# Layer 0's cross attention: the rotary turn of queries and keys moved from two TensorE products to a VectorE shuffle and a GpSimd addition

## What is computed

```python
q = (layernorm(x) @ Wq + bq).reshape(B, 100, 16, 16)
k = (ctx @ Wk + bk).reshape(B, 361, 16, 16)
v = (ctx @ Wv + bv).reshape(B, 361, 16, 16)
def _rotate_half(x):
    d = x.shape[-1] // 2
    return jnp.concatenate([-x[..., d:], x[..., :d]], axis=-1)
q = q * cos + _rotate_half(q) * sin
k = k * cos + _rotate_half(k) * sin
scores = einsum('bqhd,bkhd->bhqk', q, k) / sqrt(16)
scores = where(mask == 0, -1e30, scores)
x = x + einsum('bhqk,bkhd->bqhd', softmax(scores), v) @ Wo + bo
```

## Time and profile before

| | |
|---|---|
| median of 3 runs | 1614.06 us |
| lowest and highest run | 1605.64 and 1620.24 us |
| profiled execution, first to last instruction (span) | 1598.2 us |
| PE, DVE, ACT, POOL busy, share of the span | 90%, 48%, 41%, 9% |
| mean granted TensorE clock over the span | 0.927 |
| l0x begins, about | 166.7 us from the span's start |

### The profile page before, as it was taken

One profiled execution on the slowest core, in us unless ns is written; L12 is line 12 of the kernel. 1 busy time (PEld: TensorE's weight loads), 2 busy tenths in 40 slices (PEclk: granted clock), 3 DMA queues, 4 the chain that ended last, 5 costly groups with the idle time before them and its releaser, 6 DMA issues. The chain is left out here.

```text
span 1598.2 us, 31910 instructions
## 1 busy us (share of the span) xinstructions
PE 1442.3 (90%) x12578; PEld 1101.1 (69%) x12578; DVE 771.4 (48%) x1744; ACT 655.8 (41%) x1696; POOL 147.9 (9%) x167
## 2 busy tenths in 40 slices
PE   7999999989878899999999987998995897799897
PEld 6776667866546668777999965667884565588632
DVE  4666437755555437650000057630004587377565
ACT  3443225643256335623444424632222676156300
POOL 3000010000010110003111300021005000300000
PEclk9999999999976989999999987899997998789999
DMA  6000222001100230045899300083503000330100
GB/s 203 2 1 1 66 40 40 3 22 34 43 1 1 65 68 3 3 161 204 310 342 346 101 11 21 2 320 110 184 16 81 1 1 2 65 49 3 64 1 21
DMA packets 43581, 120.28 MB, mean 75 GB/s; under 512 B 11695, under 2 KB 28204, under 8 KB 37920
## 3 DMA queue, kind: packets, MB, share of 16 engines
q1 hardware_dynamic: 32304, 60.67, 12.7%
q0 software_dynamic: 8256, 55.02, 10.2%
q10 hardware_dynamic: 2880, 2.62, 0.5%
HBM read 95.89 MB, written 11.00 MB: 67 GB/s over the span
## 5 line engine op out<-in xcount | busy, mean ns | idle before, releaser
L756 PE MATMUL wide<-early_kt,early_q 32*100 32x361 f32 x512 | 111.1, 523 | 1.5 <-issue 0.9
L2215 ACT ACTIVATE l1f_hidden<-wide,l1f_pack 128x128 f32<-128x128 f32 x160 | 58.8, 368 | 78.0 <-PE wide L2154 68.1
L113 PE MATMUL summed<-ident 128*128 128x128 f32 x360 | 53.7, 320 | 39.0 <-PEq L66 39.0
L2317 DVE TENSOR_TENSOR l1f_out<-summed,l1f_pack 128x256 f32<-128x256 f32 x20 | 8.5, 424 | 156.7 <-PE summed L2162 156.7
L113 PEld LDWEIGHTS summed<-ident 128*128 128x128 f32 x360 | 51.8, 233 | 43.2 <-issue 43.2
L2154 PEld LDWEIGHTS wide<-l1f_rt,l1f_pack 128*128 128x128 f32 x640 | 74.5, 192 | 1.7 <-issue 0.8
L2154 PE MATMUL wide<-l1f_rt,l1f_pack 128*128 128x128 f32 x640 | 74.8, 275 | 0.6 <-ACT l1f_rt L2205 0.6
L2162 PE MATMUL summed<-l1f_pack,l1f_hidden 128*128 128x256 f32 x320 | 72.4, 379 | 0.0
L1148 DVE TENSOR_REDUCE l3x_mx<-wide 100x2 f32<-100x722 f32 x64 | 57.9, 907 | 17.1 <-PE wide L756 17.0
L2750 DVE COPY l2f_out<-summed 100x512 f32<-100x512 f32 x8 | 5.5, 691 | 125.5 <-PE summed L2650 125.5
L1148 DVE TENSOR_REDUCE l0x_mx<-wide 100x2 f32<-100x722 f32 x64 | 57.8, 907 | 16.7 <-PE wide L756 16.6
(11 more groups left out here) (588 smaller groups left out, 3396.5 us busy)
## 6 DMA issues: line engine op xcount, KB each, us to landing
l2f_w<-l2f_w_dram SPq DMA_DIRECT2D x16, 1024.0 KB, 13.6
ctxt<-ctxt_dram SPq DMA_DIRECT2D x4, 1083.0 KB, 18.1
l1f_sorted_x<-l1f_zeros SPq DMA_DIRECT2D x4, 640.0 KB
l1f_rows<-l1f_sorted_x SPq DMA_DIRECT2D x20, 128.0 KB
l1f_sorted_y<-l1f_out ACTq DMA_DIRECT2D x20, 128.0 KB, 9.1
l0f_w<-l0f_w_dram SPq DMA_DIRECT2D x18, 128.0 KB
l1f_shared<-l1f_shared_dram SPq DMA_DIRECT2D x1, 2180.0 KB
l3f_we<-l3f_we_dram SPq DMA_DIRECT2D x1, 2048.0 KB
```

Of the source, the lines that this page charges most:

```text
L113: pe.matmul(net.summed[:, 1, 0:P], net.ident[:], net.ident[:], start=True, stop=True)
L756: pe.matmul(wide[0:S, i, 0:SKV], q4[R * i:R * (i + 1), g % 2, b, g // 2, :], kt[R * i:R * (i + 1), g % 2, b, g // 2, 0:SKV], start=True, s ...
L2215: act.activation(hidden[:, f, 0:P], wide[:, f % 4, 0:P], ACT.Gelu, bias=b1_of(pack[:, n % SLOTS, :], f)).then_inc(sem["h_ready"], 1)
L2317: dve.tensor_tensor(out[:, n % 2], summed[:, n % 2, 0:E], b2_of(pack[:, n % SLOTS, :]), ALU.add).then_inc(sem["y_ready"], 1)
```

## The change

Rotation no longer uses TensorE. `rotate(kind, b)` on VectorE takes a whole turn (a batch of keys, or half of the queries, both m): it multiplies by a table of sines that already holds the signs, then by the cosines, waits for its own writes, and exchanges rows d and d + 8 of every head with one `stream_shuffle` over both m (722 or 800 columns) into a third buffer `moved`. GpSimd adds `with_cos` and `moved` (line 999 after the change) and writes keys straight to `kd`. For queries it adds in place (line 1002), then multiplies by `some`, which now holds the scale too, in two instructions (line 1007). The three buffers hold two turns each, so VectorE waits before turn n until GpSimd has finished turn n-2. The swap matrix and its transfer are gone, the ScalarE copies of rotated keys are gone, and ScalarE waits for GpSimd's last addition before it writes exponentials into l0x_pt. The units kr and qr are gone, so there are 25 units in place of 45. l1x and l3x are not touched.

```diff
-        for t in range(B + 1):
-            if t < B and not fresh:
+        for t in range(B):
+            if not fresh:
                 order += [("k", t, m) for m in range(KC)]
-            if rope and t >= 1:
-                order += [("kr", t - 1, m) for m in range(KC)]
...
-                    else:
-                        raw = unit["k" if kind == "kr" else "q", b, m]
-                        cols = SKV if kind == "kr" else COLS
-                        pe.wait_ge(unit_free[raw % 4], raw // 4 + 1)
-                        pe.matmul(bank[:, 0:cols], net.ident[:], with_cos[:, cell(*what), 0:cols], start=True, stop=False)
-                        last = pe.matmul(bank[:, 0:cols], swap[:], with_sin[:, cell(*what), 0:cols], start=False, stop=True)
...
 # ScalarE, ahead of the exponentials
                 if rope:
                     values(B - 1)
+                    act.wait_ge(sem["rotated"], len(turns_of))
...
 # GpSimd
+                def rotated(kind, b):
+                    n = place_of[kind, b]
+                    pool.wait_ge(sem["moved"], n + 1)
+                    if kind == "k":
+                        pool.tensor_tensor(kd[:, b, :, 0:SKV], with_cos[:, n % 2, :, 0:SKV], moved[:, n % 2, :, 0:SKV], ALU.add).then_inc(sem["rotated"], 1)
+                        pool.drain().then_inc(sem["k_ready"], KC)
+                        return
+                    pool.tensor_tensor(with_cos[:, n % 2], with_cos[:, n % 2], moved[:, n % 2], ALU.add)
+                    if b == 0:
+                        pool.wait_ge(sem["some_ready"], 1)
+                    pool.drain()
+                    for m in range(KC):
+                        last = pool.tensor_tensor(qt[:, b * HALF:(b + 1) * HALF, m, :], with_cos[:, n % 2, m].rearrange("p (b s) -> p b s", b=HALF),
+                                                  some[:, b * HALF:(b + 1) * HALF].unsqueeze(2).broadcast_to([P, HALF, S]), ALU.mult)
+                    last.then_inc(sem["rotated"], 1)
+                    pool.drain().then_inc(sem["q_ready"], KC)
...
+                if rope:
+                    for what in turns_of:
+                        rotated(*what)
+                        if what == ("k", 1):
+                            spread_keys(0)
+                        if what == ("k", 3):
+                            spread_keys(1)
+                        if what[0] == "q":
+                            spread_queries(what[1])
+                    spread_keys(2)
...
 # VectorE
+                def rotate(kind, b):
+                    n = place_of[kind, b]
+                    if n >= 2:
+                        dve.wait_ge(sem["rotated"], n - 1)
+                    for m in range(KC):
+                        u = unit[kind, b, m]
+                        dve.wait_ge(sem["unit_psum"], u + 1)
...
+                        dve.scalar_tensor_tensor(out=to_sin, in0=got, scalar=shift, in1=by_sin, op0=ALU.add, op1=ALU.mult)
+                        dve.scalar_tensor_tensor(out=to_cos, in0=got, scalar=shift, in1=by_cos, op0=ALU.add, op1=ALU.mult).then_inc(unit_free[u % 4], 1)
+                    dve.drain()
+                    dve.stream_shuffle(moved[:, n % 2, :, at], with_sin[:, n % 2, :, at], HALF_TURN).then_inc(sem["moved"], 1)
...
-                        dve.tensor_scalar(some[:], some[:], 0.0, None, ALU.is_gt)
+                        dve.tensor_scalar(some[:], some[:], 0.0, SCALE, ALU.is_gt, ALU.mult).then_inc(sem["some_ready"], 1)
```

More of the change, by code:

```diff
@@ L638, in rows_of @@
             return CH if c < NCH - 1 else LAST
-        def cell(kind, b, m):
-            return (KC * b + m) % 4 if kind in ("k", "kr") else 4 + m
+        turns_of = []
+        for t in range(B):
+            turns_of.append(("k", t))
+            if t in (2, 3):
+                turns_of.append(("q", t - 2))
+        place_of = {what: n for n, what in enumerate(turns_of)}
+        HALF_TURN = [i + D // 2 if i % D < D // 2 else i - D // 2 for i in range(32)]
         def values_of(b, c):
@@ L654, in _ @@
                 if rope:
[L655 removed]
+                    load_weights(sp, net, [(cos[:], dram["rope_cos"]), (sin[:], dram["rope_sin"])], sem["rope_loaded"])
                 if gate:
@@ L815, in project_context @@
                     pe.wait_ge(sem["wk_loaded"], 32 if biases else 16)
[L816 to L819, removed]
-                                project(("k", t, m))
+                    for t in range(B):
+                        net.context.wait(pe, t)
+                        for m in range(KC):
+                            project(("k", t, m))
                         if t == 1:
@@ L836, in project_context @@
                             values(t)
-                        if rope and t in (3, 4):
-                            for m in range(KC):
-                                project(("qr", t - 3, m))
                         if t in (2, 3):
@@ L897, in keys @@
                 def keys(b, m):
-                    u = unit["kr" if rope else "k", b, m]
+                    u = unit["k", b, m]
                     act.wait_ge(sem["unit_psum"], u + 1)
-                    if biases and not rope:
+                    if biases:
                         act.activation(kd[:, b, m, 0:SKV], wide[:, u % 4, 0:SKV], ACT.Identity, bias=bk[:, m:m + 1]).then_inc(unit_free[u % 4], 1)
@@ L923, in gated @@
                     last.then_inc(sem["v_ready"], 1)
-                for t in range(B + 1 if rope else B):
+                for t in range(B):
                     if rope and t == 1:
                         values(0)
-                    if rope and t >= 1:
-                        for m in range(KC):
-                            keys(t - 1, m)
                     if not rope and not fresh:
@@ L1138, in _ @@
                         dve.reciprocal(gates[:], gates[:]).then_inc(sem["gate_ready"], 1)
-                    if rope and t in (3, 4):
-                        for m in range(KC):
-                            rotated_queries(t - 3, m)
                     if t in (2, 3):
-                        for m in range(KC):
-                            queries(t - 2, m)
+                        if rope:
+                            rotate("q", t - 2)
+                        else:
+                            for m in range(KC):
+                                queries(t - 2, m)
                 def highest(n, pair):
@@ L3504, in _layouts @@
     angle = (np.arange(SKV, dtype=np.float32)[None, :] * inv[r % (D // 2)][:, None]).astype(np.float32)
-    d["rope_cos"], d["rope_sin"] = np.cos(angle), np.sin(angle)
-    swap = np.zeros((P, P), np.float32)
-    for p in range(P):
-        lower = r[p] < D // 2
-        swap[p + D // 2 if lower else p - D // 2, p] = -1.0 if lower else 1.0
-    d["rope_swap"] = swap
+    to_lower = np.where(r < D // 2, np.float32(1), np.float32(-1))
+    d["rope_cos"], d["rope_sin"] = np.cos(angle), np.sin(angle) * to_lower[:, None]
     rows = np.minimum(np.arange(PADKV), SKV - 1)
```

64 lines of the change are left out of this document (17 added, 47 removed).

## The result

The changed kernel takes 1600.69 us (median of 14 runs, 1591.53 to 1604.32) against 1614.99 us of the kernel before in 14 runs (1605.64 to 1623.16). The ratio is 0.991, with a 95% interval of 0.989 to 0.993: 14.3 us faster. The forecast was 23.7 us faster. The direction was right, the gain about three fifths of what was forecast, and the time lies inside the stated range.

A forecast was written before the change was run, and what follows sets the result against it. TensorE was taken to bound l0x's projection and the attention behind it. Removed products -24.8, hand-over +0.7 and the reduction to `some` +0.4 gave -23.7 us, so 1590.4 us, ratio 0.985; range 1580 to 1604.

The forecast's parts named there:

- The removed products: TensorE's rotation passes in l0x's projection: eight key batches and two query halves removed, 24.8 us saved.
- the hand-over's two readings: Last projection unit before l0x's first score: VectorE reads it twice, 0.59 us each, adding 0.7 us (0.5 to 1.2).
- VectorE's own time: l0x's projection: VectorE needs 3.3 us per key turn against TensorE's 5.0, 6.8 against 7.7 with queries; cost 0.
- GpSimd's additions or the shuffle cost twice the rows: Rival in l0x's projection: GpSimd needs 50 us in 45 and starts 4 us late; +9, 1599 us; chance 0.05.
- its own sign: Wrong if l0x's first product to first score exceeds 50 us, or is 46 with the end moving much less than 23.
- The sign that it named for GpSimd: In l0x's projection, VectorE waiting ahead of its products would point to GpSimd.
- GpSimd's "Cost: 0": l0x's projection: GpSimd's additions, multiplications and transfers sum to 29 us in 45; 2 us lateness is covered, costing nothing.
- The reduction to `some`: At the transposes of x, two shuffles ahead make it 1.1 us late; 0.4 us of waiting (0 to 1.1).
- The clock rival: TensorE's clock falls to 1.2 GHz at l0x's hand-over to attention, 7 us lost; 1597.4 us; chance 0.13.
- VectorE and GpSimd stand in each other's way: Rival in l0x's projection: SBUF-reading operations hold each other off; +9.2, so -14.5 us, 1599.6 us; chance 0.10.
- the middle rivals: Three cases around l0x's projection and hand-over, at 1597.4, 1599.6 and 1599 us; chances 0.13, 0.10 and 0.05.
- the port rival: VectorE and GpSimd exclude each other in l0x's projection, 4.6 us late twice; -14.5 us, 1599.6 us; chance 0.10.

The follow-up runs named there:

- e4: Changed kernel with SP issuing all l0x key and query transfers and VectorE normalising before the first rotation; ratio to before 0.9846, first product to first score 46.37 us.
- e1: Changed kernel with SP issuing all of l0x's key and query transfers, GpSimd none; ratio to before 0.9873, first product to first score 50.03 us.
- e7: As e4, but GpSimd does each key addition twice; one run, l0x's first product to first score 46.37 us.
- e2: Changed kernel with GpSimd's transfers of key batches 2 and 3 issued after the queries' second half; one run, first product to first score 49.80 us.
- e8: Changed kernel with a semaphore wait replacing the drain between GpSimd's query addition and multiplications; one run, first product to first score 51.95 us.
- e3: Changed kernel with GpSimd's first addition waiting until VectorE has normalised all eight inputs; one run, first product to first score 50.80 us.
- e0: Changed kernel unaltered, profiled a second time; one run, l0x's first product to first score 54.01 us.
- e6: Changed kernel with VectorE doing additions and query multiplications, GpSimd only issuing transfers; one run, first product to first score 55.94 us.

## Why the forecast was right in its direction and too large

**What held.** The removed products: 24.8 us forecast. e4 shows them whole: the stretch lost 70.3 - 46.4 = 23.9 us, with 0.8 paid back at the hand-over. The step of TensorE from batch 2 to the last keys was right to a tenth. The prices of shuffle and addition were right to 0.1 us, and the hand-over's two readings cost nearly what was said (1.40 us of idle in e1, e4 and e7 against 0.56 before, so 0.8 for 0.7). VectorE's own time was not short where GpSimd adds. "GpSimd's additions or the shuffle cost twice the rows" is out by their measured prices, and doubled additions cost nothing in e7 even so.

**By its own sign it failed.** It would be wrong, the prediction said, if the stretch was longer than 50 us, and it was 52.25. The sign that it named for GpSimd, VectorE waiting ahead of its products, is what the profile shows.

**The term that failed: GpSimd's "Cost: 0".** The sum of 29 us in 45 was right as busy time, and the view of who waits (VectorE for turn n-2, TensorE two turns behind) too. What the step left out is that the code drains between its operations, and that a drain behind a transfer is not free. In the 12 us from 204.81 on, the gaps behind the drains were 1.35, 3.34, 0.64 and 0.85 us; at places of the same kind with no transfer under way they are 0.71, 0.15, 0.63 and 0.19. So the holds were 0.6, 3.2, 0 and 0.7 us. This ate the two turns of slack; the forecast had counted 2 us of lateness, it was 7.0 us of waiting at VectorE, and 3.9 at the first score. e1 and e2 show it by taking the transfers away or moving them, e8 by taking one drain away. (The sum for the steepest rows is 32 us by its own terms, not 33, which changes nothing.)

**The term that was mis-sized: "The reduction to `some`".** Forecast 0.4 us of waiting at the transposes of x (up to 1.1), measured 1.7 in pauses (0.69 + 0.44 + 0.59), and 2.2 against a full gain of 2.43. The two shuffles (2 x 0.98) were in the reckoning, and with the hold gone (e3) the place costs 0.5 us, as forecast. The third part was not: GpSimd's first addition fell beside the normalising and held it for 1.4 us, which e3 removes alone. This is the mechanism of the rival "VectorE and GpSimd stand in each other's way", at a place it had not looked at. Its price was reckoned on the products with cos and sin, and these are not touched: 588 ns against 594. The Trainium skill, SBUF — State Buffer, section "Who interferes with whom", names `tensor_scalar` among the instructions that can take the ports shared with GpSimd, in the modes that use two ports, for the whole instruction. Whether these ran in such a mode no row here shows; the trace agrees with the hold: the normalising and an 8-column `tensor_scalar` beside an addition (1690 ns; 173 ns before the change) were held, the products and the shuffle, beside many additions, were not. I had cited this rule for the products only.

**The clock rival.** It came true in small. At the changed kernel's hand-over TensorE was busy 1.24 of 5 us, and then at 1.2 GHz:

```profile
220.00:225.00 5.00, 1.24 (x5) 0.43 (x3) 3.75 (x9) 0.00 (x0) 3.42 (x3) 0.96 0.12 26
225.00:230.00 5.00, 3.63 (x13) 2.19 (x14) 4.02 (x7) 0.00 (x0) 2.84 (x2) 0.50 0.00 0
```

The clock was 1.00 again at 235 to 240, with the first steps of the attention. From the first score to the next sublayer's first instruction on VectorE it took 332.39 - 226.37 = 106.0 us against 344.51 - 239.86 = 104.7 before: 1.4 us given back. The repairs do not rule this out. e4 has only the forecast's pause, its clock was 0.50 at 225 to 231, and the same distance was 106.3 us; in e1, with the same pause, it was 104.1. l0x as a whole is then 16.7 us shorter in the first profile (158.3 against 175.0 from the first product to that instruction) and 15.3 in e0. This fits the measured 14.3 us (11 to 18 by the interval of the ratio); what is left between them is smaller than the interval, and nothing was tried on it.

**The range.** It held (1580 to 1604) because the middle rivals at -14.5 to -17 were in it. That the measured -14.3 is almost the -14.5 of the port rival is luck: that sum had VectorE's products held at t = 2 and 3, which did not happen. The chance of a gain of over 1%, 0.79, was too high for a ratio of 0.991, and it was so since "Cost: 0" was given to an engine whose queue had new kinds of neighbours.

## What to carry to other kernels

Before giving an engine more work, read what stands between its operations and not only their sum: here a drain on GpSimd behind its own transfers waited for their landing, so transfers that share its queue with arithmetic were better on SP, or behind the last operation that someone waits for. When arithmetic moves to GpSimd, list the VectorE instructions of kind `tensor_scalar` that will run beside it, those that the change does not touch too; move them ahead, as here one such instruction could be held for a whole addition. And the slower engine can still be the right one: with both put right, GpSimd's additions were free even when done twice, while VectorE's, at half the price, were not (in e6, where the normalising stood at its old place).

## What the runs showed of the hardware that was not expected

- The gap for a drain on GpSimd was 0.15 us with no transfer of its own under way and up to 3.67 us behind four transfers of 91 KB. The drain ended 0.2 to 0.4 us after the last of them had landed (4.8 us from issue in the changed kernel, 2.8 in e2). With a semaphore wait at the same place the gap was 0.08 us.
- A `tensor_scalar` on VectorE from SBUF to SBUF was held while GpSimd added: 8 columns took 1690 ns, and 172 where GpSimd added nothing (e6). Products with one operand in PSUM and a table and a bias column in SBUF were not held (588 ns), nor was the shuffle (979 ns).
- The shuffle of 722 columns took 0.98 us and of 800 columns 1.07 us on 128 partitions; loading its permutation 0.01 us.
- Pauses of about 1.5 us in 5 on TensorE were followed by 1.2 GHz in e0 and e1, and pauses of 1.7 us in 5 were not in the first profile, of the same kernel as e0.
